# Half of each rotary rotation moved from the Vector engine to GpSimd

## The reference

```
h   = x mixed over channels by a per-item matrix (soft-max weighted experts) + bias
qkv = h @ w_attn.T                    # 32 heads of 32, each item attends within its 64 tokens
q, k = rope(q), rope(k)               # rope(x) = x * cos + swap_halves(x) * sin
y   = softmax(causal(q k^T)) v  +  gated attention to 10 adapter tokens
x   = x + y @ w_proj.T
c   = grouped conv1d(x, 9 taps) + context bias
x   = x + c @ W_base.T + b_base + low-rank term of 2 routed experts out of 8
```

## Time and profile before

| | |
|---|---|
| median of 3 runs | 1140.89 us (1140.59 to 1142.01) |
| span of the profiled execution | 1139.1 us |
| PE busy | 1132.2 us (99%) |
| DVE busy | 923.4 us (81%) |
| ACT busy | 359.6 us (32%) |
| POOL busy | 54.1 us (5%), 24 instructions |
| granted TensorE clock | full in every slice |

### The profile page before, as it was taken

One profiled execution on the slowest core, in us unless ns is written; L12 is line 12 of the kernel. 1 busy time (PEld: TensorE's weight loads), 2 busy tenths in 40 slices (PEclk: granted clock), 3 DMA queues, 4 the chain that ended last, 5 costly groups with the idle time before them and its releaser, 6 DMA issues.

```text
span 1139.1 us, 21477 instructions
## 1 busy us (share of the span) xinstructions
PE 1132.2 (99%) x8632; PEld 950.7 (83%) x8632; DVE 923.4 (81%) x1740; ACT 359.6 (32%) x665; POOL 54.1 (5%) x24
## 2 busy tenths in 40 slices
PE   9999999999999999999999999999999999999998
PEld 6888888888888888888888888878888888888887
DVE  5999879879889789798798799888767777877765
ACT  5433333333342432433433334323222211122210
POOL 0000000000000000000000000110000022221112
PEclk9999999999999999999999999999999999999999
DMA  6515115114125034034033177885549933233312
GB/s 222 182 56 167 67 34 162 66 53 153 56 75 167 20 97 155 12 106 146 20 111 130 45 270 269 322 251 164 185 129 347 345 89 104 96 116 116 98 38 93
DMA packets 99701, 151.81 MB, mean 133 GB/s; under 512 B 7443, under 2 KB 84115, under 8 KB 96915
## 3 DMA queue, kind: packets, MB, share of 16 engines
q1 hardware_dynamic: 98594, 135.76, 36.5%
q10 hardware_dynamic: 1008, 14.68, 3.1%
HBM read 95.88 MB, written 54.54 MB: 132 GB/s over the span
## 4 chain that ended last, share of the span: by engine, by line
PE 92%; DVE 4%; DMA 2%; issue 1%; ACT 0%; SPq 0%; DVEq 0%; ACTq 0%
PE psum L948 44%; PE psum L1026 23%; PE psum L1044 5%; PE psum L931 3%; PE psum L916 2%; PE psum L900 2%; PE psum L1078 2%; PE psum L1060 2%; PE psum L276 2%; DMA y_scratch<-a_ysb 2%; PE psum L960 2%; PE psum L909 1%; PE psum L1062 1%; PE psum L972 1%; PE psum L230 1%
## 5 line engine op out<-in xcount | busy, mean ns | idle before, releaser
L948 PE MATMUL psum<-z,w_hi 128*128 128x512 f32 x1536 | 481.5, 395 | 0.2 <-DVE z L374 0.2
L948 PEld LDWEIGHTS psum<-z,w_hi 128*128 128x128 f32 x1536 | 282.5, 188 | 57.2 <-DVE z L374 0.4
L948 PE MATMUL psum<-z,w_lo 128*128 128x512 f32 x768 | 300.5, 391 | 0.0
L1026 PE MATMUL psum<-f_wform,f_act_hi 128*128 128x512 f32 (+1 forms) x912 | 279.9, 389 | 1.3 <-DVE f_u L1494 1.1
L1026 PEld LDWEIGHTS psum<-f_wform,f_act_hi 128*128 128x128 f32 x912 | 167.9, 188 | 35.8 <-issue 2.6
L1026 PE MATMUL psum<-f_wform,f_act_lo 128*128 128x512 f32 (+1 forms) x456 | 176.2, 386 | 0.0
L948 PEld LDWEIGHTS psum<-z,w_lo 128*128 128x128 f32 x768 | 144.1, 188 | 30.6
L1026 PEld LDWEIGHTS psum<-f_wform,f_act_lo 128*128 128x128 f32 x456 | 85.7, 188 | 17.4
L875 POOL TENSOR_TENSOR f_xn<-f_x,_bbase 128x1024 f32<-128x1024 f32 x16 | 50.5, 3158 | 1009.0 <-DVE f_x L1520 678.5
L1218 ACT ACTIVATE f_act_hi<-f_act_sum 128x512 fp32r<-128x512 f32 x64 | 40.3, 632 | 119.2 <-DVE f_act_sum L1469 48.1
L1218 ACT ACTIVATE f_act_hi<-f_raw 128x512 fp32r<-128x512 f32 x56 | 33.7, 626 | 102.7 <-DVE f_raw L1552 64.8
(11 more groups left out here) (173 smaller groups left out, 1491.7 us busy)
## 6 DMA issues: line engine op xcount, KB each, us to landing
w_forms<-f_prep_lo SPq DMA_DIRECT2D x16, 896.0 KB, 5.2
f_wform<-w_forms SPq DMA_DIRECT2D x7, 2048.0 KB, 13.2
f_wform<-w_forms ACTq DMA_DIRECT2D x7, 2048.0 KB, 16.9
w_st<-in_wqkvT SPq DMA_DIRECT2D x7, 1536.0 KB, 6.3
w_forms<-f_prep_hi SPq DMA_DIRECT2D x16, 640.0 KB, 6.2
m_x<-in_x SPq DMA_DIRECT2D x16, 512.0 KB, 5.5
y_scratch<-a_ysb SPq DMA_DIRECT2D x32, 256.0 KB, 2.8
f_raw<-y_scratch SPq DMA_DIRECT2D x8, 1024.0 KB, 6.0
```

The costliest lines, as they stand in the source:

```text
L948: mm = pe.matmul(dst, w[:, c, x, :], zs, start=(c == 0 and i == 0), stop=(c == KC - 1 and i == 2))
L1026: mm = pe.matmul((prod_bank[i], bank[0])[part][:, cols], a[:, c, :], wform[i][:, w, c, cols], start=(i < 4 and c == 0 and n == 0), stop=(c ...
```

## The change

DVE does the cosine multiplication and the shuffle of each rotation, and POOL does the sine multiplication and the addition (`finish_rotation`), first K and then Q, for each of the 32 units. The turning buffer `rot` becomes two, `rot_k` and `rot_q`. A rotation on DVE now waits for POOL's addition of the same operand in the unit before, not for the other operand's. POOL's loop of 64 half rotations stands behind its three memsets and ahead of the bias additions.

```diff
-        rot = sb("rot", [P, UT])
+        rot = {K_: sb("rot_k", [P, UT])}
...
+        rot[Q_] = sb("rot_q", [P, UT])
...
+        def table(t):
+            return t[:].rearrange("p (a k) -> p a k", a=1).broadcast_to([P, UB, NC])
...
+            def finish_rotation(x, dst, n):
+                pool.wait_ge(turned[x], n + 1)
+                r = rot[x][:].rearrange("p (b k) -> p b k", k=NC)
+                pool.tensor_tensor(r, r, table(sinT), ALU.mult).then_inc(rot_step, 1)
+                pool.wait_ge(rot_step, 2 * n + (1 if x == K_ else 2))
+                half = dst[:].rearrange("p (b k) -> p b k", k=NC)
+                pool.tensor_tensor(kbd[:, :, 0:NC] if x == K_ else half, half, r, ALU.add).then_inc(rotated[x], 1)
+
+            for n in range(NG * NU):
+                finish_rotation(K_, kr, n)
+                finish_rotation(Q_, qr, n)
...
             def rotate(x, src, dst, n, used, count):
 
-                tab = [t[:].rearrange("p (a k) -> p a k", a=1).broadcast_to([P, UB, NC]) for t in (cosT, sinT)]
-                i = 0 if x == K_ else 2
                 dve.wait_ge(mm_done[x], n + 1)
-                wait(dve, rotated[Q_ if x == K_ else K_], n if x == K_ else n + 1)
+                wait(dve, rotated[x], n)
                 for s, c in used:
                     wait(dve, s, c)
                 dve.tensor_tensor(dst[:].rearrange("p (b k) -> p b k", k=NC),
-                                  src[:].rearrange("p (b k) -> p b k", k=NC), tab[0], ALU.mult).then_inc(rot_step, 1)
-                dve.stream_shuffle(rot[:], src[:], HALF_SWAP).then_inc(turned[x], 1)
-                dve.wait_ge(turned[x], n + 1)
-                r = rot[:].rearrange("p (b k) -> p b k", k=NC)
-                dve.tensor_tensor(r, r, tab[1], ALU.mult).then_inc(rot_step, 1)
-                dve.wait_ge(rot_step, 4 * n + i + 2)
-                if x == K_:
-                    dve.tensor_tensor(kbd[:, :, 0:NC], dst[:].rearrange("p (b k) -> p b k", k=NC), r, ALU.add).then_inc(rotated[x], 1)
-                else:
-                    dve.tensor_tensor(dst[:], dst[:], rot[:], ALU.add).then_inc(rotated[x], 1)
+                                  src[:].rearrange("p (b k) -> p b k", k=NC), table(cosT), ALU.mult)
+                dve.stream_shuffle(rot[x][:], src[:], HALF_SWAP).then_inc(turned[x], 1)
```

## The result

The changed kernel takes **1148.84 us** (median of 5 runs, 1147.80 to 1152.97), the kernel before 1141.43 beside it (1140.59 to 1144.37). The ratio, which is not formed from these two medians, is 1.0072, with a 95% interval of 1.0059 to 1.0085; the medians are 7.4 us apart. The profiled execution took 1147.8 us and has a span of 1146.0, 6.9 longer than that of before.

A forecast was written before the change was run, and what follows sets the result against it. PE was taken as the bound, busy 1132.2 of 1139.1 us. The span 1139.1 + 3.4 (first unit) + 5.6 (weight-preparing units) = 1148.1, plus 1.8 from span to median, gave 1149.9, stated as 1150; range 1143 to 1170.

The forecast's parts named there:

- What bounds the kernel: Whole kernel: PE is the bound, so taking 88.7 us off DVE gives back at most about 1 us.
- The price of a POOL instruction: Each 128x512 rotation instruction on POOL: taken as 1.25 us, with 0.69 and 1.55 as ends of the range.
- The bias addition's halved rate: Half of POOL's 3.09 us for a 128x1024 addition: 1.55 per rotation instruction; as a rival 1171 us, chance 0.16.
- Turns: DVE beside POOL: two-operand SBUF instructions run one after the other, the second hiding 0.13 us per handing-over.
- The prep units: 16 units that also prepare weights (u = 1 and 2): POOL's chain overruns its window by 0.35 us each, 5.6 us.
- The ledger: Step-by-step sum of a weight-preparing unit from the end of K's shuffle to the scores: 8.81 us in a window of 8.46.
- The first unit: Scores of unit 0: K's rotation on POOL waits behind the memset of vbd, so they start later; 3.4 us, once.
- The other units: Units that prepare no weights: POOL's chain of about 6.5 us is hidden in a window of 8.46; no cost.
- the last one: Last unit: next stage's first forms start 2.8 us sooner on DVE and are held up by POOL about as much.
- the new wait of PE at the scores: Sign at L900: PE waits for POOL 16 or 17 times, about 0.35 us each, one of 3 to 4 us.
- 89 us less what it loses: Sign on DVE: its busy time falls by about 89 us, less what it loses held up by POOL.

The follow-up runs named there:

- the last experiment: Changed kernel, but prep_sums reads one of its two operands from PSUM (the bank of Q's projection) instead of SBUF: 1145.88 us, ratio 1.0049.
- the first experiment: Changed kernel, but POOL finishes the rotation of K of unit 0 before it waits for the last mixing matmul and clears vbd: 1144.48 us, ratio 1.0030.

## Why the prediction was right

The forecast was 1150 us and the measured time is 1148.84; the mechanism is the one that was forecast. Point by point:

- *What bounds the kernel.* "The most that their removal can give back is about 1 us" holds: with both losses mended, DVE is relieved and the time is that of before within 0.1%. The reading under it was incomplete: beside waits of 0.4 us or less the kernel before has one of 1.5 us for DVE at the first matmuls (L230, for L319) and two of together 1.1 us in the last stage (L1026, for L1494). They stand outside the attention stage, and the runs gave nothing back there beyond 0.4 us.
- *The price of a POOL instruction.* Taken as 1.25, measured 1.28 to 1.30. The bias addition's halved rate (1.55) was too high; whether by its stepping access wasn't tested. The estimate from the Trainium skill ("GPSIMD Engine Reference", Performance versus the Vector engine), 1.12, was too low by an eighth. By that figure alone there would have been no overrun in the prep units.
- *Turns.* Two-operand SBUF instructions excluded each other as rows 6 said, and one-operand ones did not; the last experiment shows it for the sums. The Trainium skill ("SBUF — State Buffer", Who interferes with whom) states the rule: a DVE instruction with two SBUF inputs contends with a GpSimd instruction that reads SBUF, one with at most one SBUF input, outside the 2-port perf modes, doesn't. The trace agrees, 935 ns against 424.
- *The prep units.* The ledger ended at 8.81, the trace at 8.60: POOL's K instructions ended at 1.43 and 2.87 instead of 1.55 and 2.94, Q's shuffle at 4.87 instead of 5.02, Q's at 6.86 and 8.55 instead of 7.06 and 8.66, and the way to PE took 0.05 instead of 0.15. (The ledger's second sum, 0.27, should have been 0.29 like its third, which changes nothing.) The overrun is 0.15 instead of 0.35 us per unit. The first prep unit has none, since the slow clock holds PE up longer than POOL; without it that unit overruns by 0.7 us, since it has a split of z that the ledger left out. In sum it is 2.4 us instead of 5.6. Since the overrun is the small difference of two long chains, an error of 2% in the chain was over half of the term.
- *The first unit.* The wait came out as forecast to 0.1 us. The term, 3.4, was 4.8 in the trace, counted from the clearing of vbd to the scores of unit 1 (89.66 - 60.54 against 85.05 - 60.71): the slow clock behind the wait (1.3) was left out. It was in no row of the kernel before. Of these 1.3 us, 0.6 are net, since the clock hides the first prep unit's overrun.
- *The other units* and the last one: no cost, as said; one unit was 0.3 longer. In the u = 3 units POOL was done 3.1 to 3.4 us ahead of the scores (2.3 in the last), where the forecast left 2.0.

The two misses, 3.2 too much in the prep units and 1.4 too little at the start, partly cancelled; that the sum was better than its terms was luck. Of what was to be seen, the new wait of PE at the scores, forecast 16 or 17 times with 0.35 us, is there 16 times, but only 0.1 us long where it isn't the first, so that the list of PE's waits names only the first. And DVE's busy time fell by 15 us instead of "89 us less what it loses": the loss was five sixths of it, and would have misled a reader who takes busy time for work.

## What to carry to other kernels

Work moved to a slower engine is paid on the path from its input to whoever waits for its output, so look for the shortest such window and for what stands ahead in the new engine's queue, not at the shares of busy time. Beside GpSimd, order VectorE's queue so that what GpSimd waits for comes first and two-operand SBUF work that nobody waits for comes last: one line swapped was worth 2.9 us here. When PE is the bound, look at the granted clock behind every new wait of a microsecond or more: the wait can cost more than its length, and it can also hide another loss.

## What the runs showed of the hardware

A wait of 4.1 us left PE at half its clock for over 3 us, 1.3 to 1.5 us on top (distances between scores of 21.89, 21.93 and 22.05 us in three kernels, against 20.56). Of 15 waits of 1.75 to 1.79 us in one run, six were followed by half the clock, 1.6 us on top each, paid by six units that waited for nobody themselves; nine were not, and what decides isn't shown. Waits of 1.30 us (once) and of 0.78 and 0.53 us (in the first experiment) left it at 1.00, as did those of some 0.1 us in the changed kernel's prep units. Sixteen matmuls on constant data in the gap of 4.1 us kept it up.

POOL's 128x512 multiplication and addition of two SBUF operands took 1.28 to 1.30 us undisturbed, 1.9 times DVE's 0.69. Beside them, a DVE instruction with two SBUF operands waited for its turn and was shown as busy meanwhile (935 ns instead of 422); with one operand in PSUM it took 424 ns.
